# Relative attention over four batches: each tile's round trip to HBM in even and odd rows in place of column halves

## The chip, the cores and the metric

The program runs on one core of a Trainium2 chip. The metric is the device time of one execution in microseconds, from the first to the last instruction of that core, as a median over runs. The engines are TensorE (PE; its weight loads are PEld), VectorE (DVE), ScalarE (ACT), GpSimd (POOL), and SyncE (SP), which here only waits and issues DMAs.

## What is computed

Four batch elements of 2048 tokens with 256 channels pass through attention A, a feed-forward layer, attention B (causal) and the feed-forward layer again, each with a layer norm ahead and a residual sum behind. The change lies in attention A, which has 16 heads of 16 channels and a relative position score:

```python
content_score = einsum('bhsp,bhtp->bhst', q + u, k)
pos_score = einsum('bhsp,htp->bhst', q + v, pos)
x = pad(pos_score, ((0,0),(0,0),(0,0),(1,0)))          # a zero ahead of each row
pos_score = x.reshape(b, h, s + 1, s)[:, :, 1:, :].reshape(b, h, s, s)
weights = softmax((content_score + pos_score) / sqrt(P))
out = einsum('bhst,bhtp->bhsp', weights, val)
```

The relative shift is a change of row length: rows of 2049 floats (a zero and 2048 scores) are laid end to end, the first 2048 floats are dropped, and the rest is cut into rows of 2048.

## The kernel before, in words

One loop over the batch elements runs ten phases with a barrier between them; attention A is one of them. A head's 2048 x 2048 scores are worked in 16 tiles of 128 rows (`NT`), so a batch element has 256 tiles and the program 1024. On each engine `in_order` (line 491) writes out the steps by hand: step s works on several tiles at once, each part of the work some tiles ahead (`R_LEAD` 9, `Z_LEAD` 6, `C_LEAD` 4, `T_LEAD` 2, `V_LEAD` 1).

A tile n goes through these parts:

- **Position scores.** In step n-9, PE makes the 128 x 2048 scores in four matmuls of 512 columns (`rows_of`, line 516), in the order of columns 3, 0, 1, 2. DVE copies chunk 3 from PSUM into `rel` (line 693), ACT chunks 0, 1 and 2 (line 639). Each copy raises `r_copied[c]`. `rel` has four slots (`RING`).
- **Write.** In the same step SP writes the tile to `rel_rows` in HBM, in two DMAs of 512 KB (`write_half`, line 762). Row i of a head starts there at float i*2049 + 1, so that the row of 2049 with its zero comes about. Both DMAs raise `rel_out[slot]` by 16.
- **Read.** In step n-6 SP reads the shifted tile back into `z` (four slots), again as two DMAs of 512 KB (`read_half`, line 756); row i starts at float (i+1)*2048. Ahead of them `read_ready` (line 743) waits until the last transposes of tile n-4 have read the slot (`t_full[3]`, done by PE in this same step) and until both writes of tile n and of tile n+1 have landed. Both reads raise `rel_in[slot]`.
- **Scores.** In step n-4 PE makes the content scores, and DVE adds `z` and takes the maximum, in two halves (`score`, line 646; the custom instruction of line 658). It starts when both reads have landed. POOL subtracts the maximum (line 716).
- **Softmax and values.** In step n-2 PE transposes the tile (`turn`, line 538), ACT takes the exponential, and one step later PE multiplies with the values.

SP's queue is one order for everything: in a step it issues read half 0 of tile s+6, write half 0 of tile s+9, read half 1, write half 1 (`step`, lines 797 to 802), and behind them, in 12 of 16 steps, two loads of 64 KB for the next heads and in one step a load of 256 KB (`next_heads`, line 771; `load_part`, line 720, puts 16 rows into partitions six apart). A DMA that SP has not issued holds back all behind it. Before the change a half is 128 rows by 1024 columns: 128 pieces of 4 KB. Write half 0 waits for `r_copied[1]` (columns 0 to 1023), write half 1 for `r_copied[3]` and `r_copied[2]`:

```python
for c in ((R_DVE, R_ACT[-1]) if half else (R_ACT[1],)):
    e.wait_ge(r_copied[c], e.snap(base.tiles + (n + 1)))
```

PE waits for the same copies: its chunk 0 of the next tile's scores comes only after DVE's copy of chunk 3 (line 599), and DVE makes that copy behind its first half of `score`.

Two pieces of code outside of attention A come up below. At the start of the program the constant `embT` is loaded (128 partitions, two rows of 8 KB each), and then `k_sb` (zero there) is written from 48 partitions, 4 KB each, to two places of `qu_parts` and two of `k_parts`. Ahead of each attention A 24 loads of 64 KB fill the first heads' operands, by `load_part`.

Of the kernel before, what the change touches and what calls it, by code (L numbers as in the profile page):

```python
# [26 lines left out]
P = 128  # L27
# [4 lines left out]
S = 2048  # L32
NT = S // P
# [9 lines left out]
FLAT = S * (S + 1)  # L43
RING = 4
# [10 lines left out]
R_ACT = [0, 1, 2]  # L55
R_DVE = 3
R_FIRST = 3
HB = 4
NB = 2
# [20 lines left out]
def program(nc, a, out, nb=4, nh=H):  # L80

    ctx = ExitStack()
    with ctx:
        def sb(name, shape, dt=F32):
            return ctx.enter_context(nc.sbuf_tensor(name, shape, dt))
# [4 lines left out]
        def sem(name):  # L90
            return ctx.enter_context(nc.semaphore(name))
# [8 lines left out]
        rel_d = nc.dram_tensor("rel_rows", (NB, FLAT), F32).ap()  # L100
# [8 lines left out]
        rel = sb("rel", [P, RING, S])  # L109
        z = sb("z", [P, RING, S])  # L110
# [104 lines left out]
        r_copied = [sem(f"r_copied{c}") for c in range(4)]  # L215
        rel_out = [sem(f"rel_out{k}") for k in range(RING)]
        rel_in = [sem(f"rel_in{k}") for k in range(RING)]
# [13 lines left out]
        def settle(e):  # L231

            e.sem_inc(waited, 1)
# [257 lines left out]
        def in_order(e, b, step):  # L491

            def counts(p):
                return Counts(*(e.snap(b * (nh // HB * per) + p * per)
                                for per in (G, G // OB, 32 * G // RING, HB // NB * QK_INC, HB // NB * 16)))

            with e.Fori(0, 1) as p:
                base = counts(p)
                for s in range(-R_LEAD, 0):
                    step(p, base, s, lambda n: n >= 0)  # L500
            with e.Fori(0, GROUPS - 1) as p:
                base = counts(p)
                for s in range(G):
                    step(p, base, s, lambda n: True)
            with e.Fori(GROUPS - 1, GROUPS) as p:
                base = counts(p)
                for s in range(G):
                    step(p, base, s, lambda n: n < G)

        def moved(base, n):  # L510

            return base.moves + 32 * (n // RING + 1)
# [212 lines left out]
        def load_pair(e, q, k, q_src, k_src, h, slots, done):  # L725

            for a in slots:
                load_part(e, q, q_src, h, a, QPART[a], done)
                load_part(e, k, k_src, h, a, KPART[a], done)

        def load_v(e, h, hd, done):
            e.dma_start(v_s[hd].rearrange("p t w -> p (t w)"),
                        v_d[bass.ds(h, 1)].rearrange("a p w -> (a p) w")).then_inc(done, 16)

        def sp_attn_a(e, b):

            every = range(SLOTS)
            load_pair(e, qv_s[0], pos_s[0], qv_d, pos_d, 0, every, qv_loaded[0])
            load_pair(e, qu_s[0], k_s[0], qu_d, k_d, 0, every, AA["qk_loaded0"])
            load_v(e, 0, 0, AA["v_loaded0"])  # L740
            load_pair(e, qv_s[1], pos_s[1], qv_d, pos_d, 1, every, qv_loaded[1])

            def read_ready(p, base, n, fresh, last):

                k = n % RING
                if not fresh:

                    e.wait_ge(t_full[3], e.snap(base.tiles + (n - RING + 1)))
                    settle(e)
                e.wait_ge(rel_out[k], e.snap(moved(base, n)))  # L750
                settle(e)
                if not last:
                    e.wait_ge(rel_out[(n + 1) % RING], e.snap(moved(base, n + 1)))
                    settle(e)

            def read_half(n, half):

                k, hd, i0, c0 = n % RING, n // NT % NB, n % NT * P, half * S // 2
                shifted = bass.AP(tensor=rel_d.tensor, offset=hd * FLAT + (i0 + 1) * S + c0, ap=[[S, P], [1, S // 2]])
                e.dma_start(z[:, k, c0:c0 + S // 2], shifted).then_inc(rel_in[k], 16)  # L760

            def write_half(base, n, half):

                k, hd, i0, c0 = n % RING, n // NT % NB, n % NT * P, half * S // 2
                for c in ((R_DVE, R_ACT[-1]) if half else (R_ACT[1],)):
                    e.wait_ge(r_copied[c], e.snap(base.tiles + (n + 1)))
                    settle(e)
                there = bass.AP(tensor=rel_d.tensor, offset=hd * FLAT + i0 * (S + 1) + 1 + c0, ap=[[S + 1, P], [1, S // 2]])
                e.dma_start(there, rel[:, k, c0:c0 + S // 2]).then_inc(rel_out[k], 16)

            def next_heads(p, base, s, final):

                hd, at = s // NT, s % NT
                nxt = (hd + 1) % NB
                if at in range(1, 7) and not (final and hd + 1 >= HB):
                    if at == 1:
                        e.wait_ge(AA["hi_ready"], e.snap(base.tiles + hd * NT + C_LEAD))
                        settle(e)
                    load_pair(e, qu_s[nxt], k_s[nxt], qu_d, k_d, e.snap(p * HB + (hd + 1)), (at - 1,),
                              AA[f"qk_loaded{nxt}"])  # L780
                if at == 7 and not (final and hd + 1 >= HB):
                    e.wait_ge(AA["pv_done"], e.snap(base.tiles + (hd * NT + V_LEAD)))
                    settle(e)
                    load_v(e, e.snap(p * HB + (hd + 1)), nxt, AA[f"v_loaded{nxt}"])
                if at in range(8, 14) and not (final and hd + 2 >= HB):
                    if at == 8:
                        e.wait_ge(r_full[2], e.snap(base.tiles + (hd + 1) * NT))
                        settle(e)
                    load_pair(e, qv_s[hd % NB], pos_s[hd % NB], qv_d, pos_d, e.snap(p * HB + (hd + 2)), (at - 8,),
                              qv_loaded[hd % NB])  # L790

            def step(p, base, s, here):

                n, r = s + Z_LEAD, s + R_LEAD
                final = not here(G)
                if here(n):
                    read_ready(p, base, n, s < 0 and n < RING, n % NT == NT - 1)
                for half in range(2):
                    if here(n):
                        read_half(n, half)  # L800
                    if here(r):
                        write_half(base, r, half)
                if s >= 0:
                    next_heads(p, base, s, final)

            in_order(e, b, step)
# [642 lines left out]
```

## Time and profile before

| | |
|---|---|
| median of 3 runs | 11098.51 us (11085.86 to 11107.45) |
| profiled execution | 11115.23 us |
| its span, first to last instruction | 11113.4 us |
| busy share: PE, PEld, DVE, ACT, POOL | 85%, 60%, 56%, 60%, 26% |
| mean granted clock of TensorE | 0.947 |
| bytes moved by DMA | 2482 MB, 223 GB/s over the span |

The page of the profile is of one execution. Its rows give busy time by group of instructions, waits with what ended them, and for DMA the packets, their bytes and the share of time in which the core's 16 DMA engines had a packet under way; that share can come out a little over 100%, since a packet is counted as begun a few ns before the one ahead of it has ended. The profiled execution is 16.7 us above the median, and the same events make up both.

### The profile page before, as it was taken

The page shows a single profiled execution, that of the slowest core. Times are in us where ns is not written, and L with a number is a line of the kernel's source. Part 1 is how long each engine was busy: PE and PEld are TensorE (multiplying, and loading weights), DVE is VectorE, ACT ScalarE, POOL GpSimd, SP SyncE. Part 2 cuts the span into 40 slices and gives each one's busy share as a digit, 9 for nine tenths or more (in the row PEclk, how much of TensorE's full clock was granted, in tenths as well). Part 3 has the DMA queues.
Part 4 walks back from the last instruction along what each step waited for, and adds up shares of the span by engine and source line. Part 5 has one row for each costly group of instructions (what it writes and reads, how often), then busy time and mean ns, then how long its engine had stood idle before and what let it go on. Part 6 is the DMA issues. An engine that isn't in the chain of part 4 may idle for free. (4 is left out here: it accounts for less than half of the span.)

```text
span 11113.4 us, 271423 instructions
## 1 busy us (share of the span) xinstructions
PE 9422.7 (85%) x95520; PEld 6711.5 (60%) x95520; DVE 6258.0 (56%) x14730; ACT 6687.5 (60%) x11009; POOL 2944.3 (26%) x3520
## 2 busy tenths in 40 slices
PE   5888888999688888899968888889996888888999
PEld 3665665666465666566646656656663565665666
DVE  3655663765365566376446556637644565663764
ACT  3666663765466666376546666637644666663764
POOL 2333332001233333200123333310012333331001
PEclk7999999999899999999989999999998999999999
DMA  6999992000699999100069999911007999991100
GB/s 240 378 363 366 381 378 87 26 25 16 233 377 366 361 379 380 59 25 25 16 254 380 367 362 382 365 46 27 23 18 265 373 372 362 379 357 48 27 22 26
DMA packets 747623, 2482.45 MB, mean 223 GB/s; under 512 B 111745, under 2 KB 133761, under 8 KB 745921
## 3 DMA queue, kind: packets, MB, share of 16 engines
q1 hardware_dynamic: 746176, 2463.84, 60.3%
q8 instruction: 826, 13.53, 0.5%
q14 instruction: 621, 5.08, 0.1%
HBM read 1280.34 MB, written 1183.07 MB: 222 GB/s over the span
## 5 line engine op out<-in xcount | busy, mean ns | idle before, releaser
L658 DVE CUSTOM_DVE_ANT_0 z<-sc,z 128x1024 f32<-128x1024 f32 x2048 | 2496.5, 1220 | 1848.5 <-DMA z<-rel_rows 1608.0
L716 POOL TENSOR_SCALAR z<-z,nmax 128x1024 f32<-128x1024 f32 x2048 | 2277.8, 1123 | 4028.5 <-DVE nmax L668 4028.5
L631 ACT ACTIVATE pT<-rg 128x512 f32<-128x512 f32 x4096 | 2445.9, 598 | 738.7 <-PE rg L541 679.5
L541 PE MATMUL rg<-ident,z 128*128 128x128 f32 x16384 | 2527.0, 277 | 77.0 <-issue 68.3
L639 ACT ACTIVATE rel<-rg 128x512 f32<-128x512 f32 x3072 | 1721.1, 596 | 1407.2 <-PE rg L522 1401.8
L541 PEld LDWEIGHTS rg<-ident,z 128*128 128x128 f32 x16384 | 1990.3, 142 | 784.6 <-ACT rel L639 294.4
L522 PE MATMUL rg<-pos_s,qv_s 96*128 96x512 bf16 x4096 | 1590.8, 396 | 1021.4 <-DVE rel L693 901.6
L1013 DVE CUSTOM_DVE_ANT_0 z<-sc,mask 128x1024 f32<-128x1024 f32 (+7 forms) x1536 | 1359.1, 910 | 227.0 <-PE sc L832 173.9
L952 ACT ACTIVATE pT<-rg 128x512 f32<-128x512 f32 (+3 forms) x1792 | 928.4, 550 | 763.0 <-PE rg L885 751.0
L522 PEld LDWEIGHTS rg<-pos_s,qv_s 96*128 96x128 bf16 x4096 | 478.7, 118 | 1498.0 <-DVE rel L693 1150.9
L960 ACT ACTIVATE z<-z,nmax 128x128 f32<-128x128 f32 (+15 forms) x1024 | 1226.6, 1198 | 89.0 <-POOL nmax L978 76.7
L885 PE MATMUL rg<-ident,z 128*128 128x128 f32 x8704 | 1256.8, 289 | 0.0
L562 PE MATMUL op<-pT,xnT 128*32 128x128 f32 x32768 | 1129.9, 279 | 0.0
L885 PEld LDWEIGHTS rg<-ident,z 128*128 128x128 f32 x8704 | 972.0, 145 | 254.9 <-issue 188.4
L562 PEld LDWEIGHTS op<-pT,xnT 128*32 128x32 f32 x32768 | 847.2, 111 | 243.9 <-issue 214.0
L866 PE MATMUL op<-pT,xnT 128*32 128x128 f32 x17408 | 791.9, 283 | 149.6 <-ACT pT L952 45.5
L693 DVE COPY rel<-rg 128x512 f32<-128x512 f32 x1024 | 702.4, 686 | 183.1 <-PE rg L522 142.4
L866 PEld LDWEIGHTS op<-pT,xnT 128*32 128x32 f32 x17408 | 503.2, 110 | 299.1 <-DVE attn L988 120.6
L534 PE MATMUL sc<-k_sb,xnT 96*128 96x512 bf16 x2048 | 631.2, 390 | 0.0
L534 PE MATMUL sc<-xnT 96*128 96x512 bf16 x2048 | 615.1, 381 | 0.7 <-DVE mlo L658 0.7
L1032 DVE COPY pT<-rg 128x512 f32<-128x512 f32 (+3 forms) x768 | 428.6, 558 | 297.3 <-PE rg L885 288.2
L700 DVE COPY po_sb<-op 128x128 f32<-128x128 f32 x1024 | 298.8, 292 | 494.1 <-PE op L562 493.2
(93 smaller groups left out, 8161.5 us busy)
## 6 DMA issues: line engine op xcount, KB each, us to landing
rel_rows<-rel SPq DMA_DIRECT2D x2048, 512.0 KB, 7.2
z<-rel_rows SPq DMA_DIRECT2D x2048, 512.0 KB, 7.1
xnT<-qu_parts SPq DMA_DIRECT2D x792, 64.0 KB, 2.3
xnT<-v_heads SPq DMA_DIRECT2D x132, 256.0 KB, 4.3
v_heads<-rel SPq DMA_DIRECT2D x8, 4096.0 KB, 12.5
k_sb<-k_parts SPq DMA_DIRECT2D x408, 64.0 KB, 2.3
qv_s<-qv_parts SPq DMA_DIRECT2D x384, 64.0 KB, 6.2
pos_s<-pos_parts SPq DMA_DIRECT2D x384, 64.0 KB, 7.2
```

The lines of the kernel that those rows point to most:

```text
L522: e.matmul(rg[:, R_BANK[c], :], qv_s[hd][:, i0:i0 + P], pos_s[hd][:, c * CH:(c + 1) * CH], start=True, stop=True).then_inc(r_full[c], 1)
L534: mm = e.matmul(sc[:, c, :], qu_s[hd % NB][:, i0:i0 + P], k_s[hd % NB][:, c * CH:(c + 1) * CH], start=True, stop=True)
L541: mm = e.transpose(rg[:, T_BANK[q], (j - 4 * q) * P:(j - 4 * q + 1) * P], z[:, n % RING, j * P:(j + 1) * P], ident[:, :])
L562: mm = e.matmul(po[32 * g:32 * g + 32, :], v_s[hd % NB][:, j, :], pT[:, n % 2, j * P:(j + 1) * P], start=j < 4, stop=j + 4 >= NT)
L631: e.activation(pT[:, t % 2, q * CH:(q + 1) * CH], rg[:, T_BANK[q], :], ACT.Exp, scale=SCALE).then_inc(p_ready[q], 1)
L639: e.activation(rel[:, r % RING, c * CH:(c + 1) * CH], rg[:, R_BANK[c], :], ACT.Copy).then_inc(r_copied[c], 1)
L658: e.tensor_tensor_reduce(out=zs, in0=scf[:, 2 * half * CH:2 * (half + 1) * CH], in1=zs, scale=1.0, scalar=-3.0e38, op0=ALU.add, op1=ALU.ma ...
L716: e.tensor_scalar(zs, zs, 1.0, nmax[:, n % 2:n % 2 + 1], ALU.mult, ALU.add).then_inc(AA[done], 1)
L866: mm = e.matmul(po[32 * g:32 * g + 32, :], v_s[t // NT % NB][:, j, :], pT[:, t % 2, j * P:(j + 1) * P], start=j < 4, stop=j + 4 >= nj)
L885: mm = e.transpose(rg[:, B_BANK[q], (j - 4 * q) * P:(j - 4 * q + 1) * P], z[:, t % RING, j * P:(j + 1) * P], ident[:, :])
L960: e.activation(z[:, s % RING, 0:w], z[:, s % RING, 0:w], ACT.Exp, bias=nmax[:, s % 2:s % 2 + 1], scale=SCALE).then_inc(BB["exp_done"], 1)
L1013: e.tensor_tensor_reduce(out=z[:, s % RING, c0:c1], in0=scf[:, p0:p0 + c1 - c0], in1=mask[:, S - width + c0:S - width + c1], scale=1.0, sc ...
```

## The change

A half is no longer 1024 columns of all 128 rows but all 2048 columns of 64 rows: half 0 is the even rows of the tile, half 1 the odd ones, for the write and for the read. A DMA then has 64 pieces of 8 KB where it had 128 of 4 KB; it still carries 512 KB. Write half 0 now waits for the whole tile (`r_copied[3]` and `r_copied[2]`), write half 1 for nothing. The order in which SP issues them, the semaphores and their counts stay.

```diff
             def read_half(n, half):
 
-                k, hd, i0, c0 = n % RING, n // NT % NB, n % NT * P, half * S // 2
-                shifted = bass.AP(tensor=rel_d.tensor, offset=hd * FLAT + (i0 + 1) * S + c0, ap=[[S, P], [1, S // 2]])
-                e.dma_start(z[:, k, c0:c0 + S // 2], shifted).then_inc(rel_in[k], 16)
+                k, hd, i0 = n % RING, n // NT % NB, n % NT * P
+                shifted = bass.AP(tensor=rel_d.tensor, offset=hd * FLAT + (i0 + 1 + half) * S, ap=[[2 * S, P // 2], [1, S]])
+                e.dma_start(z[half:P:2, k, :], shifted).then_inc(rel_in[k], 16)
 
             def write_half(base, n, half):
 
-                k, hd, i0, c0 = n % RING, n // NT % NB, n % NT * P, half * S // 2
-                for c in ((R_DVE, R_ACT[-1]) if half else (R_ACT[1],)):
-                    e.wait_ge(r_copied[c], e.snap(base.tiles + (n + 1)))
-                    settle(e)
-                there = bass.AP(tensor=rel_d.tensor, offset=hd * FLAT + i0 * (S + 1) + 1 + c0, ap=[[S + 1, P], [1, S // 2]])
-                e.dma_start(there, rel[:, k, c0:c0 + S // 2]).then_inc(rel_out[k], 16)
+                k, hd, i0 = n % RING, n // NT % NB, n % NT * P
+                if half == 0:
+                    for c in (R_DVE, R_ACT[-1]):
+                        e.wait_ge(r_copied[c], e.snap(base.tiles + (n + 1)))
+                        settle(e)
+                there = bass.AP(tensor=rel_d.tensor, offset=hd * FLAT + (i0 + half) * (S + 1) + 1, ap=[[2 * (S + 1), P // 2], [1, S]])
+                e.dma_start(there, rel[half:P:2, k, :]).then_inc(rel_out[k], 16)
```

## Rows read from the trace of the kernel before

**Rows 1.** The page: packets of the whole span.

```profile
DMA packets 747623, 2482.45 MB, mean 223 GB/s; under 512 B 111745, under 2 KB 133761, under 8 KB 745921
```

**Rows 2.** Windows, the four stretches of attention A: times, busy, clock, DMA share, GB/s.

```profile
181.00:1696.00 1515.00, 1276.72 (x14597) 910.79 (x14597) 901.18 (x1894) 1002.25 (x1765) 562.74 (x506) 0.98 1.00 373
2935.00:4453.00 1518.00, 1283.67 (x14593) 915.67 (x14594) 901.01 (x1894) 1001.84 (x1765) 562.74 (x506) 0.97 1.00 372
5700.00:7210.00 1510.00, 1275.17 (x14593) 910.33 (x14594) 900.58 (x1894) 1001.78 (x1765) 562.80 (x506) 0.98 1.00 374
8467.00:9985.00 1518.00, 1278.43 (x14595) 911.89 (x14596) 900.99 (x1894) 1001.68 (x1765) 562.78 (x506) 0.97 1.00 373
```

**Rows 3.** Waits over the whole span: who waited for whom, us, times, longest.

```profile
DVE z L658 <- DMA z<-rel_rows: 1608.0, 905, 10.6
...
PE rg L522 <- DVE rel L693: 901.6, 989, 9.6
```

**Rows 4.** DMA, 200 to 1690 us: GB/s in 40 slices, packets, the queue.

```profile
GB/s 371 391 390 372 376 372 389 376 366 377 289 373 351 382 387 385 375 374 376 392 372 285 392 366 382 389 379 381 369 376 378 392 385 372 387 378 384 366 368 382
DMA packets 158334, 556.84 MB, mean 374 GB/s; under 512 B 21898, under 2 KB 21898, under 8 KB 158125
...
q1 hardware_dynamic: 158125, 554.14, 99.6%
```

**Rows 5.** DMA, 18 to 21 us: the load of embT, rows of 8 KB.

```profile
DMA packets 177, 1.25 MB, mean 418 GB/s; under 512 B 11, under 2 KB 25, under 8 KB 25
...
q1 hardware_dynamic: 177, 1.25, 100.4%
```

**Rows 6.** DMA, 182 to 185 us: writes of rel_rows alone, 4 KB each.

```profile
DMA packets 330, 1.22 MB, mean 407 GB/s; under 512 B 32, under 2 KB 32, under 8 KB 330
...
q1 hardware_dynamic: 330, 1.22, 101.7%
```

**Rows 7.** Timeline, one tile: start, us, what, idle before it.

```profile
1005.16 1.09 ACT L639 ACTIVATE rel<-rg 128x512 f32<-128x512 f32 x2 [1.15 <-PE rg L522]
...
1006.34 0.33 SPq L769 DMA_DIRECT2D rel_rows<-rel  x1
...
1006.72 0.61 SPq L760 DMA_DIRECT2D z<-rel_rows  x1
1006.85 0.60 ACT L639 ACTIVATE rel<-rg 128x512 f32<-128x512 f32 x1 [0.61 <-PE rg L522]
...
1007.54 0.62 SPq L769 DMA_DIRECT2D rel_rows<-rel  x1
...
1009.09 0.60 PE L541 MATMUL rg<-ident,z 128*128 128x128 f32 x4
...
1010.45 0.56 SPq L760 DMA_DIRECT2D z<-rel_rows  x1
...
1011.60 0.33 SPq L769 DMA_DIRECT2D rel_rows<-rel  x1
...
1012.80 0.78 SPq L769 DMA_DIRECT2D rel_rows<-rel  x1
```

**Rows 8.** DMA issues: count, KB each, median us to landing.

```profile
rel_rows<-rel SPq DMA_DIRECT2D x2048, 512.0 KB, 7.2
z<-rel_rows SPq DMA_DIRECT2D x2048, 512.0 KB, 7.1
xnT<-qu_parts SPq DMA_DIRECT2D x792, 64.0 KB, 2.3
...
qu_parts<-k_sb SPq DMA_DIRECT2D x2, 192.0 KB, 10.8
```

**Rows 9.** Line 760, the reads: landing times of all 2048.

```profile
DMA to landing us min/median/max: 3.8/7.1/9.9
```

**Rows 10.** DMA, 22.2 to 23.2 us: writes out of 48 partitions (k_sb).

```profile
DMA packets 120, 0.39 MB, mean 385 GB/s; under 512 B 28, under 2 KB 28, under 8 KB 112
```

**Rows 11.** DMA, 160 to 172 us: loads into 16 partitions, six apart.

```profile
q1 hardware_dynamic: 604, 1.24, 40.4%
```

## The prediction

> **What bounds the kernel now.** I read the page first. Its DMA row shows that nearly all packets are under 8 KB [rows 1], and its slices show four stretches in which the DMA engines are full and four in which they are nearly idle. So I took the windows of the four full stretches, which are attention A: 1515, 1518, 1510 and 1518 us, 6061 us in all, with a DMA share of 1.00 and 372 to 374 GB/s in each, while PE is busy for 84% at a granted clock of 0.97 to 0.98 [rows 2]. Over 1024 tiles that is 5.92 us a tile. The waits say that the DMA is also what ends last: DVE waited for the read of `z` ahead of line 658 in 905 tiles, 1608 us in all, and PE waited 901.6 us in 989 tiles for the copy that DVE makes behind that [rows 3]. TensorE would be faster by about 0.9 us a tile if the reads came at once. The reader is to see a closed loop: 99.6% of the time of 16 DMA engines is taken [rows 4], the queue is filled as far as the four slots of `z` and `rel` allow, and compute runs at the rate of the landings. So a cheaper byte shortens the stage, and a busier compute engine would not lengthen it.
>
> Half of the change acts on the price of a byte, the other half on when the DMAs are issued.
>
> **The pieces of 8 KB.** A tile moves 2 MiB (2.097 MB), a write and a read of 1 MiB; with the head loads it is 374 times 5.92, some 2.21 MB. The trace has both sizes of piece under a full queue. While `embT` is loaded, 152 of the 177 packets are 8 KB and they carry all of the 1.25 MB, at 418 GB/s [rows 5]; so a row of 8 KB is one packet and isn't cut in two. While `rel_rows` is written alone, in 4 KB pieces, it is 407 GB/s [rows 6]. That is 2.6% less time for a byte. The 2.097 MB take 5.61 us at 374 GB/s, and 2.6% of that is 0.148 us a tile.
>
> The bounds. The mixture of reads and writes runs at 374, not at 407 GB/s, and what takes the difference isn't in a row: 0.996 times 1490 us times 16 engines over 136,227 packets of over 512 B is 174 ns each [rows 4], against 48.8 us over 298 packets, 164 ns, in writes alone [rows 6]. If those 10 ns belong to the packet and not to its bytes, 16 packets fewer on each DMA engine and tile save 0.16 us more, 0.31 in all. If the mixture is bound by the memory behind the engines, the size of a piece gains nothing: 0. I take 0.148, nearest to the rows that show both sizes; nothing shows that the stalls go by the packet.
>
> The Trainium skill (DMA: Bandwidth & Descriptors, "Why small descriptors are slow (HBM only)") puts the fixed overhead of a packet inside a DMA engine at some 3 cycles, of a fabric of 850 MHz: 3.5 ns, so 16 fewer would save 0.06 us a tile. By it alone the gain here would be 58 us, not 151.
>
> **The later issue.** Write half 0 waited for columns 0 to 1023 and now waits for the last copy. In the timeline it is issued at 1006.34, behind ACT's first two copies (1005.16 to 1006.25), and write half 1 at 1007.54, behind the copy that runs from 1006.85 to 1007.45; one tile on it is 1011.60 and 1012.80 [rows 7]. So write half 0 moves back by 1.2 us. Queued behind it on SP are read half 1 (at 1006.72 now, so 1007.9), write half 1 (then 1008.5 or so), the two head loads of 12 steps in 16, and the next read half 0, which was issued at 1010.45 although its transposes (from 1009.09 for 0.60 us) had been done for 0.8 us; it will be some 1 us later. All four of a tile's DMAs so shift by up to 1.2 us against compute. DVE waits for the landing of read half 1, PE for DVE.
>
> What hides it is the queue. A DMA of 512 KB lands 7.1 us (median) after its issue; one of 64 KB outside of the stretch takes 2.3 us [rows 8]; 512 KB at 374 GB/s are 1.4 us. So some 3.4 us of older work stand ahead of a DMA when it is issued. With 1.2 us off, 2.2 us are left, and the engines go on without a gap. But this is a median: the reads land after 3.8 to 9.9 us [rows 9], and 3.8 is a queue with nothing in it. Where less than 1.2 us stands ahead, the engines will run dry.
>
> The bounds here: nothing, if the queue always covers it; and 0.6 us a tile, if the queue is used up. The latter: a slot of `z` comes round in four periods, of which two are compute behind the scores (n-4 to n-2), so that 1.2 us more in the loop would be borne by two periods. A gain is excluded, since nothing is issued sooner but by the one wait that SP saves, and SP has idle time. I take a price from the slices: 3 of the 40 are at 289, 351 and 285 GB/s where the rest are at 362 to 392 [rows 4], so in one tile of 13 the queue is short already; each of them pays 1.2 us, 0.09 us a tile.
>
> Costed at nothing: a DMA's issue on SP (four of a tile, 0.33 to 0.8 us each, no more pieces than before); the landings, since both halves of a read and both writes of tiles n and n+1 were waited for before as well; DVE, ACT, PE, POOL, whose instructions don't change. Cover for all is the DMA queue; were it gone, PE would be next, at about 5.0 us a tile.
>
> **The sum.** -0.148 + 0.09 = -0.058 us a tile, times 1024: -59 us. The profiled execution took 11115.2, 16.7 above the median of 11098.5; taken from the latter, 11040 us, 0.5% less. A change within 0.2%, 22 us, is about what can't be told from none.
>
> **Rivals.**
>
> *A: the stalls go by the packet.* Then it is -0.31 + 0.09 = -0.22 us a tile, -225 us: 10873. For it: a larger piece has fewer starts. Against it: the same 4 KB pieces, written alone, take 164 ns, so it is the mixture that stalls and not the start of a piece. 0.11.
>
> *B: the two terms cancel*, or the mixture is bound by memory and the queue covers the delay: 11077 to 11120. 0.19 with the flank of the forecast.
>
> *C: the delay decides.* The place is write half 0's wait on SP, with read half 1 behind it. Should half of the 0.6 us come through, it is +0.30 - 0.148 = +0.15 us a tile, +156: 11254. The point from which it turns: more than 0.148 us a tile, an eighth of the 1.2 us. For it: 16 DMA engines don't run evenly, and a landing waits for the last; the queue of the slowest tiles is empty now. Against it: 99.6%, and 3.4 us ahead in the median. 0.22.
>
> *D: half of the partitions.* A DMA now reads or fills every second partition. If DMA engines get in each other's way on the SBUF side, the price shows in two places. The writes out of 48 partitions ran at 385 GB/s [rows 10], so the writing half should be safe. The loads into 16 partitions six apart took 0.404 times 12 times 16, 77.6 us for 1.24 MB [rows 11], 62.6 ns for 1000 bytes against 40.0 in rows 6: 1.56 times. If that were all from sharing, and the reads (1.05 MB, 2.8 us a tile) took 1.56 times as long, it is +1.6 us a tile. But each of those loads is a single piece for a DMA engine on an empty queue, so a first access is in it; and four pieces an engine spread over more places. I take a quarter of it, 0.4 us: 11040 + 410 = 11450. It turns from 0.06 us, 2% of the reads' time. 0.15.
>
> *That 8 KB rows are cut in two*, so that the change isn't what it says, is excluded by rows 5.
>
> **How the numbers follow.** The forecast has 0.33 as a gain of over 0.2%, and A 0.11: faster 0.44. B gives same 0.19. C 0.22 and D 0.15: slower 0.37. The likeliest case's own range is 10945 to 11110 (a gain of 0.12 to 0.18 us a tile, a loss of 0.03 to 0.13). The range over the cases goes from A's 10873 to C's 11254; D and the outermost bounds are left out, 2 in 10.
>
> **What the profile after would show.** Packets of 8 KB in attention A, some 260,000 of them, and a mean GB/s of 376 to 380 in the four stretches at a DMA share still at 0.98 or more: the forecast. Write half 0 behind the third copy of line 639, and a median landing about 1 us shorter: the delay as told. A share down to 0.95 with the stage no shorter: C. A share still at 1.00 and GB/s well under 370: D, and the time per 8 KB packet far over 330 ns. GB/s near 390: A. I am wrong if the stage moves while the GB/s don't, or if PE's waits on DVE's copy don't follow the stage.

## The result: 4.7% slower, and the profile after

The changed kernel takes 11616.35 us (median; 11610.57 to 11665.41) against 11102.98 us before: a ratio of 1.0466, with a 95% interval of 1.0447 to 1.0484. That is 513 us more, where 59 us less was forecast.

All of it lies in attention A. The windows of its four stretches after (start:end, length, busy us with counts of PE, PEld, DVE, ACT and POOL, granted clock, DMA share, GB/s):

```profile
181.00:1826.00 1645.00, 1328.44 (x14609) 946.20 (x14609) 902.71 (x1898) 1005.82 (x1767) 562.93 (x507) 0.94 0.96 344
3075.00:4717.00 1642.00, 1331.64 (x14642) 949.70 (x14643) 904.18 (x1901) 1006.53 (x1768) 563.99 (x508) 0.94 0.96 345
5948.00:7587.00 1639.00, 1325.05 (x14644) 944.35 (x14645) 904.10 (x1902) 1006.21 (x1768) 564.11 (x508) 0.95 0.96 346
8829.00:10483.00 1654.00, 1343.44 (x14637) 957.67 (x14641) 904.52 (x1900) 1007.59 (x1768) 564.11 (x508) 0.93 0.96 342
```

These are 6580 us against 6061 [rows 2]. The windows of before end 4 to 6 us ahead of a stage's last landing, those of after at most 2, so a stage is better taken from the first issue of its DMAs of `rel_rows` to their last landing (from the trace): 6583 us against 6083, 500 us more, 6.43 us a tile for 5.94. The two profiled executions differ by 496 us. The DMA share is 0.96 where it was 1.00, the rate 342 to 346 GB/s where it was 372 to 374. The engines do the same work (DVE, ACT and POOL are busy as long as before); TensorE's mean granted clock is 0.93 to 0.95 where it was 0.97 to 0.98, and the same matmuls keep it busy for 4% longer (1328 us for 1277 in the first stretch); it waits longer than before all the same.

The DMA view of 200 to 1690 us after, and the waits over the span:

```profile
DMA packets 86786, 511.78 MB, mean 343 GB/s; under 512 B 20386, under 2 KB 20386, under 8 KB 27586
...
q1 hardware_dynamic: 86595, 509.30, 95.5%
```

```profile
DVE z L658 <- DMA z<-rel_rows: 1843.8, 820, 10.7
...
PE rg L522 <- DVE rel L693: 1186.9, 953, 9.7
```

The pieces are what the change says: of 86,786 packets only 27,586 are under 8 KB. But the engines have a packet under way for 95.5% of the time in place of 99.6% [rows 4], and the waits of PE behind the read have grown from 901.6 to 1186.9 us [rows 3].

The issues over the whole span (count, KB, median us from issue to landing), and all times of the reads:

```profile
rel_rows<-rel SPq DMA_DIRECT2D x2048, 512.0 KB, 6.6
z<-rel_rows SPq DMA_DIRECT2D x2048, 512.0 KB, 6.5
```

```profile
L760 SPq DMA_DIRECT2D z<-rel_rows x2048: 450/588/2194, 187.2 to 10478.2; - x187
...
DMA to landing us min/median/max: 3.7/6.5/9.0
```

The landing after the issue is 0.6 us shorter than before, 6.5 for 7.1 [rows 8]. And the issue itself is slower: at least 450 ns on SP, where the forms of 128 rows took at least 314 (shown below). In the timeline of one tile after, the issue order can be read off as in rows 7:

```profile
1008.93 0.52 SPq L760 DMA_DIRECT2D z<-rel_rows  x1
...
1009.41 0.60 ACT L639 ACTIVATE rel<-rg 128x512 f32<-128x512 f32 x1 [0.61 <-PE rg L522]
...
1010.10 0.49 SPq L770 DMA_DIRECT2D rel_rows<-rel  x1
...
1010.64 0.59 SPq L760 DMA_DIRECT2D z<-rel_rows  x1
...
1011.02 1.23 DVE L658 CUSTOM_DVE_ANT_0 z<-sc,z 128x1024 f32<-128x1024 f32 x1 [1.61 <-DMA z<-rel_rows]
...
1011.28 1.25 SPq L770 DMA_DIRECT2D rel_rows<-rel  x1
...
1012.17 0.69 DVE L693 COPY rel<-rg 128x512 f32<-128x512 f32 x1
...
1015.03 0.60 ACT L639 ACTIVATE rel<-rg 128x512 f32<-128x512 f32 x1 [0.61 <-PE rg L522]
...
1016.85 0.59 SPq L760 DMA_DIRECT2D z<-rel_rows  x1
```

Read half 0 is issued at 1008.93, then SP stands until ACT's last copy has ended (1010.01) and sends write half 0, read half 1 and write half 1 in one burst. The last three lines show what the wait hangs on: DVE copies chunk 3 behind its first half of `score` (1011.02), ACT's last copy ends 4.61 us after the start of that `score`, and only then does the next read half 1 go out.

### The profile page after: what moved, and what is told of

It is laid out like the page before. It is cut to its first block and busy times, and to the rows that moved or that the text cites. A ratio compares the mean times of both kernels' runs of the same rounds, so it can differ in the third digit from the quotient of the medians.

```text
span 11609.5 us, 270399 instructions
## 1 busy us (share of the span) xinstructions
PE 9622.3 (83%) x95520; PEld 6849.9 (59%) x95520; DVE 6257.9 (54%) x14730; ACT 6698.1 (58%) x11009; POOL 2939.1 (25%) x3520
## 5 line engine op out<-in xcount | busy, mean ns | idle before, releaser
L522 PE MATMUL rg<-pos_s,qv_s 96*128 96x512 bf16 x4096 | 1633.6, 406 | 1307.1 <-DVE rel L693 1186.9
L541 PE MATMUL rg<-ident,z 128*128 128x128 f32 x16384 | 2581.5, 281 | 86.1 <-issue 77.4
L541 PEld LDWEIGHTS rg<-ident,z 128*128 128x128 f32 x16384 | 2051.6, 145 | 816.4 <-ACT rel L639 262.5
L886 PE MATMUL rg<-ident,z 128*128 128x128 f32 x8704 | 1257.4, 289 | 0.0
L562 PE MATMUL op<-pT,xnT 128*32 128x128 f32 x32768 | 1215.2, 293 | 0.0
L886 PEld LDWEIGHTS rg<-ident,z 128*128 128x128 f32 x8704 | 971.8, 145 | 254.7 <-issue 188.1
L562 PEld LDWEIGHTS op<-pT,xnT 128*32 128x32 f32 x32768 | 903.9, 116 | 259.7 <-issue 209.0
L867 PE MATMUL op<-pT,xnT 128*32 128x128 f32 x17408 | 791.7, 283 | 149.5 <-ACT pT L953 45.5
L867 PEld LDWEIGHTS op<-pT,xnT 128*32 128x32 f32 x17408 | 503.1, 110 | 298.9 <-DVE attn L989 120.4
```

The source lines that it names most:

```text
L522: e.matmul(rg[:, R_BANK[c], :], qv_s[hd][:, i0:i0 + P], pos_s[hd][:, c * CH:(c + 1) * CH], start=True, stop=True).then_inc(r_full[c], 1)
L541: mm = e.transpose(rg[:, T_BANK[q], (j - 4 * q) * P:(j - 4 * q + 1) * P], z[:, n % RING, j * P:(j + 1) * P], ident[:, :])
L562: mm = e.matmul(po[32 * g:32 * g + 32, :], v_s[hd % NB][:, j, :], pT[:, n % 2, j * P:(j + 1) * P], start=j < 4, stop=j + 4 >= NT)
L867: mm = e.matmul(po[32 * g:32 * g + 32, :], v_s[t // NT % NB][:, j, :], pT[:, t % 2, j * P:(j + 1) * P], start=j < 4, stop=j + 4 >= nj)
L886: mm = e.transpose(rg[:, B_BANK[q], (j - 4 * q) * P:(j - 4 * q + 1) * P], z[:, t % RING, j * P:(j + 1) * P], ident[:, :])
```

## The experiments

Each kernel was timed against the kernel before on the same chip. There were two theories at the start: **delay** (what the new wait holds up costs the time) and **sharing** (DMA engines get in each other's way when every second partition is used). Once delay had held, the question was what part of it counts.

### Shapes alone, and each part alone

**b1_bench.** Ahead of the last constant load of the kernel before, eight blocks of 4 MiB, each alone on the queue:

```diff
+            for k in range(RING):
+                for h in range(2):
+                    move(flat(k * P + h, 2, P // 2, S, S), z[h:P:2, k, :])
+            landed()
...
+            for k in range(RING):
+                for h in range(2):
+                    move(z[h:P:2, k, :], flat(k * P + h, 2, P // 2, S, S))
+            landed()
```

> The kernel before, with eight blocks of DMAs ahead of its last constant load, each block of 4 MiB in itself and alone on the queue: first written to HBM, then read back, as column halves (128 pieces of 4 KB), even and odd rows (64 of 8 KB), upper and lower 64 rows (64 of 8 KB) and whole tiles (128 of 8 KB). Two theories. Sharing: DMA engines that fill or drain every second partition get in each other's way on the SBUF side. Then the reads in even and odd rows run well under those of column halves (at 350 GB/s or less against 400), those of 64 rows on end at about half, near 210, and whole tiles at 410 to 420; the writes may show it or not. Delay: the shape isn't at fault. Then every block runs at 395 to 420 GB/s, the ones of 8 KB pieces some 2% above column halves.

The DMA view inside the blocks, written first (column halves, even and odd rows, upper and lower 64, whole), then read in the same order:

```profile
DMA packets 1000, 3.64 MB, mean 404 GB/s; under 512 B 112, under 2 KB 112, under 8 KB 1000
```
```profile
DMA packets 576, 3.80 MB, mean 422 GB/s; under 512 B 112, under 2 KB 112, under 8 KB 112
```
```profile
DMA packets 593, 3.88 MB, mean 298 GB/s; under 512 B 120, under 2 KB 120, under 8 KB 120
```
```profile
DMA packets 504, 3.74 MB, mean 415 GB/s; under 512 B 48, under 2 KB 48, under 8 KB 48
```
```profile
DMA packets 1092, 3.99 MB, mean 363 GB/s; under 512 B 117, under 2 KB 117, under 8 KB 1092
```
```profile
DMA packets 621, 4.05 MB, mean 368 GB/s; under 512 B 127, under 2 KB 127, under 8 KB 127
```
```profile
DMA packets 624, 4.07 MB, mean 214 GB/s; under 512 B 127, under 2 KB 127, under 8 KB 127
```
```profile
DMA packets 550, 4.10 MB, mean 410 GB/s; under 512 B 50, under 2 KB 50, under 8 KB 50
```

These windows cut the blocks at different places; that of the even and odd reads takes in both idle ends of its block. From the first packet's start to the last one's end, worked out from the trace, the four shapes are written at 399, 413, 287 and 412 GB/s and read at 339, 358, 217 and 370. Either way even and odd rows are no slower than column halves. Sharing is there, but for another shape: 64 rows on end. So sharing falls as the cause. That each block would run at 395 to 420 GB/s, as delay had it, missed for all reads and for 64 rows on end. (This single execution took 11219.88 us, 111 us above the kernel before, about the time of the blocks.)

**e1_late_wait.** The waits alone; column halves stay.

```diff
-                for c in ((R_DVE, R_ACT[-1]) if half else (R_ACT[1],)):
-                    e.wait_ge(r_copied[c], e.snap(base.tiles + (n + 1)))
-                    settle(e)
+                if half == 0:
+                    for c in (R_DVE, R_ACT[-1]):
+                        e.wait_ge(r_copied[c], e.snap(base.tiles + (n + 1)))
+                        settle(e)
```

> Column halves as before; only the waits are those of the changed kernel (write half 0 waits for the whole tile, write half 1 for nothing). Delay: most of the loss of 513 us is here, 11400 to 11620 us. Sharing: only the 0.09 us a tile of the prediction, 11100 to 11200 us.

Measured 11483.23 us against 11109.11, ratio 1.0326 (1.0291 to 1.0361): 374 of the 513 us with no change of shape. Delay holds.

**e2_read_rows.** Reads in even and odd rows, nothing else.

```diff
...
-                e.dma_start(z[:, k, c0:c0 + S // 2], shifted).then_inc(rel_in[k], 16)
+                e.dma_start(z[half:P:2, k, :], shifted).then_inc(rel_in[k], 16)
```

> Only the reads are even and odd rows; the writes are column halves with the early wait. Delay: no loss, since nothing is issued later: 11000 to 11110 us. Sharing on the side that fills SBUF: 11400 to 11620 us.

Measured 11065.45 us, ratio 0.9956 (0.9943 to 0.9970): 0.4% faster. The half of the change that adds no wait is a gain.

**e3_write_rows.** Writes in even and odd rows with their late wait, reads as before.

```diff
...
-                e.dma_start(there, rel[:, k, c0:c0 + S // 2]).then_inc(rel_out[k], 16)
+                e.dma_start(there, rel[half:P:2, k, :]).then_inc(rel_out[k], 16)
```

> Only the writes are even and odd rows, with the late wait; the reads are column halves. Delay: 11400 to 11620 us. Sharing on the side that fills SBUF: 11050 to 11200 us. Should it be slow while the column halves with the late wait are not, the writes share too.

Measured 11643.94 us, ratio 1.0476 (1.0439 to 1.0513). That is a little above both ranges. With the late wait the row writes add 161 us to e1. With the gain of the row reads, 44 us by e2, the parts come to 374 + 161 - 44 = 491 of the 513 us.

### What is late: the write or the read behind it

Write half 0's wait holds up the write, and read half 1 behind it on SP. Four orders of issue tell which counts.

**e8_cols_late_reads_first.** e1 with both reads issued first; **e7_rows_reads_first**, the same edit on the changed kernel; **e10_before_reads_first**, on the kernel before.

```diff
                 for half in range(2):
                     if here(n):
                         read_half(n, half)
+                for half in range(2):
                     if here(r):
                         write_half(base, r, half)
```

> Column halves with the late wait (11483 us in the run before), but SP issues both reads first and then both writes, so that only the writes stand behind the wait. Theory 1, the late read: the loss comes from read half 1 queued behind write half 0's wait; then it goes, 11050 to 11200 us. Theory 2, the late write: the pause ahead of write half 0 and the burst behind it drain the queue whatever the order; then it stays at 11400 us or more.

Measured 11102.34 us against 11121.49, ratio 0.9990 (0.9976 to 1.0004). The late wait is still there and costs next to nothing (this order without the late wait, e10 below, is 0.13% better by its ratio, about 15 us): the 374 us were read half 1 standing behind it.

> The changed kernel with both reads issued ahead of both writes. Late read: 11000 to 11200 us, and a little under the column halves in this order, by the larger pieces. Late write: 11500 us or more. If it stays some 150 us above the column halves in this order, the writes in even and odd rows have a cost of their own.

Measured 11000.10 us, ratio 0.9896 (0.9877 to 0.9916): the changed kernel, with its reads out of the way of the wait, is 1.0% faster than before, and 102 us under e8. Here the size of the pieces shows by itself.

> The kernel before, early wait and column halves kept, with both reads issued ahead of both writes. Late read: read half 1 gains 1.5 to 2 us against compute, but the DMA engines were already full, so little is left to gain: 11050 to 11130 us. If a full queue still left stalls in the reads, it is 11000 us or less; if alternating reads and writes had a worth of its own, 11150 us or more.

Measured 11078.94 us against 11113.10, ratio 0.9977 (0.9964 to 0.9989). Sooner than before brings next to nothing; later costs much.

**e9_read1_last.** The kernel before, both of its waits kept, read half 1 issued last.

```diff
-                for half in range(2):
-                    if here(n):
-                        read_half(n, half)
+                if here(n):
+                    read_half(n, 0)
+                for half in range(2):
                     if here(r):
                         write_half(base, r, half)
+                if here(n):
+                    read_half(n, 1)
```

> The kernel before, both early and late waits kept, with read half 1 issued behind write half 1 in place of between the writes: the read is late by 0.8 to 1.6 us and no write is later. Late read: 11300 to 11600 us. Late write: 11050 to 11200 us.

Measured 11961.10 us, ratio 1.0754 (1.0731 to 1.0776). No write is later behind its `score` than before, and the loss is the largest of these orders, 840 us, above what was expected of either theory. The late read is shown from both sides. The DMA view of its 200 to 1690 us:

```profile
DMA packets 138892, 487.56 MB, mean 327 GB/s; under 512 B 19442, under 2 KB 19442, under 8 KB 138708
...
q1 hardware_dynamic: 138708, 485.18, 98.9%
```

This is the row to remember: a share of 98.9% at 327 GB/s, where before it was 99.6% at 374 [rows 4]. The same pieces take longer: 0.989 times 1490 us times 16 engines over the 119,266 packets of over 512 B is 198 ns each, for 174 before. In e3, where the size tells the direction, it is the reads that are stretched: from 300 to 1600 us its 4 KB packets, all of them reads (some 4,800 of 55,700 are loads for the next heads), took 199 ns in the mean, and its 8 KB writes 325, so 162 for 4 KB (means worked out from the trace's packets). A packet counts as under way while it is stretched, so a full share doesn't say that the queue holds work in advance.

### How much, by how late

**e13_read_ahead_of_write.** Column halves; read half 1 behind the wait, but ahead of write half 0. `write_ready` is the late wait of e1, taken out of `write_half`.

```diff
+                if here(n):
+                    read_half(n, 0)
+                if here(r):
+                    write_ready(base, r)
+                if here(n):
+                    read_half(n, 1)
                 for half in range(2):
-                    if here(n):
-                        read_half(n, half)
                     if here(r):
                         write_half(base, r, half)
```

> Column halves; read half 1 still behind the wait for the last copy, but issued ahead of write half 0. It comes 0.38 us sooner than with the late wait alone, and with 512 KB less ahead of it on the queue. Late read, by time of issue alone: a third of 374 us less, 11330 to 11420 us. If the write ahead of it on the queue is what it waits for: 11150 to 11300 us. If the wait alone is the matter: 11483 us still.

Measured 11317.13 us against 11116.04, ratio 1.0181 (1.0158 to 1.0204), between the two ranges given.

**e12_late_and_pause.** e1 with a pause on SP behind write half 0.

```diff
+                if half == 0:
+                    for _ in range(6):
+                        settle(e)
```

> Column halves with the late wait (11483 us), and six more semaphore increments on SP between write half 0 and read half 1, a pause of some 0.3 us that moves nothing but the issues behind it. It stands for the slower issue of the 64-row forms, which in the run with the writes in even and odd rows puts read half 1 later by some 0.3 us. If the lateness of read half 1 is all of that run's 160 us above the late wait: 11580 to 11720 us. If the 8 KB writes cost something of their own: 11480 to 11540 us.

Measured 11550.75 us, ratio 1.0385 (1.0362 to 1.0407): 67 us over e1, under the one range and 11 us over the other.

For these runs I worked out of the trace, for the tiles between 300 and 1600 us, the mean time from the start of DVE's first half of `score` to the end of SP's issue of read half 1 in the same step, and the time from there to the `score` that this read feeds, which is two tiles on. The two add up to two periods (the time of a tile), by construction; what the table shows is how a later issue is shared out between them. The loss is that against the kernel before, timed beside it:

| run | `score` to issue of read half 1 | from there to its own `score` | period | loss |
|---|---|---|---|---|
| e10, reads first | 3.54 us | 8.21 us | 5.88 us | -34 us |
| e8, reads first, late wait | 3.64 us | 8.30 us | 5.97 us | -19 us |
| before | 4.41 us | 7.51 us | 5.96 us | 0 |
| e13 | 5.14 us | 7.29 us | 6.21 us | 201 us |
| e1 | 5.71 us | 6.94 us | 6.32 us | 374 us |
| e12 | 6.00 us | 6.84 us | 6.42 us | 435 us |
| e3 | 6.17 us | 6.87 us | 6.52 us | 535 us |
| changed kernel | 6.21 us | 6.74 us | 6.48 us | 513 us |
| e9 | 6.04 us | 7.54 us | 6.79 us | 840 us |

A read that is issued 0.8 to 0.9 us sooner than before (e10, e8) lands sooner by next to nothing: the second column grows by 0.7 to 0.8. One that is issued later makes up for less than half of it: e1 is 1.30 us later and wins back 0.57, and half of the 0.73 left is 0.365 us a tile, 374 us. The runs from e13 down to the changed kernel cost 274 to 304 us for each microsecond of later issue. e9 is off this line, at 515: it is 1.63 us later and wins back nothing. It has both writes ahead of the late read; no run shows whether that is the reason.

The first column hangs on compute. ACT's last copy ends 4.61 us (median) after the start of `score` in every run of the table; where the late read stands behind that copy, `score`, the copies, SP's issue and the landing are one closed loop of two periods. TensorE's clock goes into its length. In e1, 31 of the 206 tiles had a matmul of the position scores that took over 500 ns, at the lower of the clock's two levels; ACT's last copy ended 5.5 us behind `score` there, not 4.6, and the issue of read half 1 at 6.44 us, that of the others at 5.58. Before, it is 13 of 218 tiles. No run takes the clock apart from the wait.

**e14_rows_read_ahead.** e13's order on the changed kernel.

> The changed kernel, all in even and odd rows, with read half 1 issued behind the wait for the last copy but ahead of write half 0 (the same with column halves: 11317 us). If 8 KB pieces are cheaper wherever the read is in time, and the writes in rows cost only by standing ahead of the late read, it is at or under that, 11200 to 11320 us. If writes in rows have a cost of their own once the read is late, 11360 us or more.

Measured 11200.64 us against 11122.86, ratio 1.0068 (1.0051 to 1.0084): 1.1% under the same order in column halves, so row writes have no cost of their own that shows. In e3 and in the changed kernel they cost because write half 0 stands between the wait and the late read, and SP takes longer over it: the issue of read half 1 ends 0.46 us later in e3 than in e1, which at the 274 to 304 us above is some 130 of the 161 us. A part of that is the issue of the write itself; the issues of e1 and of the changed kernel's form in e3 (min, median, max ns):

```profile
L770 SPq DMA_DIRECT2D rel_rows<-rel x2048: 314/448/1643, 180.5 to 10366.0; - x187
```
```profile
L770 SPq DMA_DIRECT2D rel_rows<-rel x2048: 450/516/2329, 180.2 to 10507.9; - x187
```

The 64-row form takes 136 ns more at the least. It goes by the number of rows and not by their length or the step: whole tiles of 128 rows by 8 KB were issued in 314 ns too (e6), 64 rows on end, without the step of two, in 460 (e4).

### A kernel that beats both

**e5_read_whole.** The kernel before with a tile's reads made one DMA.

```diff
+                if half:
+                    return
...
+                e.dma_start(z[:, k, :], shifted).then_inc(rel_in[k], 16)
```

> The kernel before, with the two reads of a tile made one of 128 rows by 8 KB (1 MiB), issued where read half 0 was; writes as before. Late read: the read is complete on the queue 2.2 us sooner and has the larger pieces (-0.4% in the run with the reads in even and odd rows), so 10950 to 11070 us. Late write: as that run, 11020 to 11110 us. Should the alternation of halves matter by itself, it is above 11150 us.

Measured 11023.30 us against 11121.49, ratio 0.9907 (0.9889 to 0.9924). That lies in the ranges of both theories and doesn't tell them apart.

**e11_whole_read_row_writes.** The same read, and the changed kernel's writes.

> The read of a tile as one DMA of 1 MiB ahead of the writes, and the writes in even and odd rows with the late wait: all pieces 8 KB, nothing to be read stands behind the wait. Late read, with the larger pieces as a gain: 10930 to 11030 us, at or under the changed kernel with its reads first (11000 us). Late write: above 11100 us.

Measured 10967.18 us against 11113.10, ratio 0.9866 (0.9842 to 0.9890): the fastest. Its DMA view from 300 to 1600 us:

```profile
DMA packets 80196, 493.60 MB, mean 380 GB/s; under 512 B 16106, under 2 KB 16106, under 8 KB 23114
...
q1 hardware_dynamic: 80011, 491.20, 98.4%
```

The share is 98.4%, below that of before, at 380 GB/s.

**e6_whole_both.** One write of 1 MiB too.

```diff
...
+                there = bass.AP(tensor=rel_d.tensor, offset=hd * FLAT + i0 * (S + 1) + 1, ap=[[S + 1, P], [1, S]])
+                e.dma_start(there, rel[:, k, :]).then_inc(rel_out[k], 16)
```

> One read and one write of 1 MiB for a tile, 128 rows by 8 KB, the write behind the late wait. If only the read's place and the size of the pieces count: 10930 to 11050 us, as the run beside it. If the halving of the write matters, because the next read waits for the landing of both writes of the next tile, it is 11100 us or more.

Measured 11508.45 us, ratio 1.0359 (1.0336 to 1.0383), as slow as with a late read, but the read isn't late behind `score`: its issue ends 3.36 us behind it in the mean, in e11 3.21. SP's own waits from 200 to 1600 us (us, times, longest), e6 first, e11 second:

```profile
SPq L233 <- DMA rel_rows<-rel: 430.6, 196, 5.9
```
```profile
SPq L233 <- DMA rel_rows<-rel: 104.8, 104, 3.4
```

`read_ready` waits for the landing of the next tile's write, and a write of 1 MiB lands later (10.7 us in the median, where e11's halves take 7.9). The loop then goes through the write: from `score` to the write's issue 4.82 us, to its landing 10.61, to the read's issue 0.28, to the read's own `score` 9.38 (means from the trace), 25.1 us in all, which is four periods; in e11 the same way takes 23.4. No run took this wait out, so that it is the cause is read from the trace and not shown by a run.

**e4_top_bottom_rf.** e7 with the upper and the lower 64 rows as halves.

```diff
...
-                e.dma_start(z[half:P:2, k, :], shifted).then_inc(rel_in[k], 16)
+                e.dma_start(z[half * (P // 2):(half + 1) * (P // 2), k, :], shifted).then_inc(rel_in[k], 16)
```

> The changed kernel with its reads first (11000 us), but its halves are the upper and the lower 64 rows in place of even and odd ones. Alone on the queue these ran at 287 GB/s written and 217 read against 413 and 358 for even and odd rows. Sharing on the SBUF side: the mixture falls from 379 to between 250 and 330 GB/s, 11800 to 13500 us. If reads and writes in alternation hide it: under 11300 us.

Measured 12558.31 us, ratio 1.1311 (1.1283 to 1.1339), against 0.9896 for even and odd rows. So sharing is dear in the kernel too where the shape has it, and even and odd rows don't have it.

## Why the prediction was wrong

**The direction.** Faster was forecast, with 0.37 on slower; 11616 lies above the range. The time came from rival C, to which I gave 0.22 and 156 us.

**The bound of the stretch** was read rightly in one way: the reads' landing ends last, and the loop passes what it costs to PE. It was read wrongly in another: that 99.6% of the engines' time was taken, "the queue is filled", and so a shift of the issue would be hidden. e9 has 98.9% at 327 GB/s.

**The pieces of 8 KB: right in direction, too large by 29 to 48%.** I priced them at -0.148 us a tile, -151 us. With the read in time they brought 102 us (e8 to e7), with the read half late 117 (e13 to e14), in reads alone 44 (e2). The estimate from the overhead of a packet that the Trainium skill gives (DMA: Bandwidth & Descriptors, "Why small descriptors are slow (HBM only)"), 58 us, is too low, by 43 to 50%. Rival A isn't seen.

**The later issue: the step that failed.** "What hides it is the queue", with 3.4 us ahead and 1.2 us taken off, priced at 0.09 us a tile. The wait alone measures 374 us, 0.365 a tile (e1). The 3.4 us were the median landing less that of a quiet load, and I took all of it for older work that can be used up. The landing of reads tells how much really was: it went from 7.1 [rows 8] to 6.6 us in e1:

```profile
rel_rows<-rel SPq DMA_DIRECT2D x2048, 512.0 KB, 6.9
z<-rel_rows SPq DMA_DIRECT2D x2048, 512.0 KB, 6.6
```

So of 1.2 us later only 0.5 came back as a shorter landing, and the rest reached DVE. For read half 1 alone the table has 1.30 us later, 0.57 back and 0.73 left, and spread over two periods that is the 374 us. The cover was mis-sized, since a minimum of 3.8 us [rows 9] was the sign that I set aside as rare.

The upper bound of 0.6 us a tile held, but its loop was the wrong one, and that the factor of two came out is luck. I had the slot of `z` come round in four periods, two of them compute. But in the changed kernel SP hardly waits for that slot (`t_full[3]`, PE's line 541). Its waits for it (us, times, longest), first before, from 180 to 1695 us, then in the changed kernel, from 200 to 1600 us:

```profile
SPq L233 <- PE rg L541: 137.2, 124, 6.0
```
```profile
SPq L233 <- PE rg L541: 17.4, 12, 6.6
```

The loop that closes is `score`, DVE's copy of chunk 3, PE's chunk 0 of that same tile (not of the next, as I wrote ahead), ACT's copies, SP, the read, and the `score` two tiles on: a late read holds up the very copy that the next late read waits for.

The price of 0.09 us had no ground either. Two of the three low slices of [rows 4] fall on single pauses of 14 us, where the loop over groups of 64 tiles turns (tile 68's `score` starts at 604.7 us, 14.57 after the one ahead; tile 132's at 991.0, 14.08 after it), and tell nothing of a short queue in one tile of 13.

**"Costed at nothing: a DMA's issue on SP".** This was wrong too: 450 ns at the least in place of 314. By the table the later issue of read half 1 accounts for some 130 of the 161 us between e1 and e3. A pause on SP, 0.29 us of later issue, costs 67 (e12), and e14 shows no such cost where the write isn't ahead of the read.

**Rival D: excluded for this shape**, by the blocks (422 and 368 GB/s) and by e7. Why the loads six apart [rows 11] were dear, no run told. The Trainium skill (SBUF — State Buffer, "Door 1: The DMA port swizzle") gives some 218 GB/s for 64 partitions on end: the reads agree with 214, the writes ran at 298 and don't. What I had worked out from its rule for even and odd rows, reads twice as long, is not seen.

**Of the signs given** the one for C was right: a share of 0.955 with the stage no shorter. The landing was to be 1 us shorter and is 0.6; had I asked what follows from anything less than 1.2, the rival would have had its price.

## What to carry to other kernels

Before a DMA is put behind a longer wait, look at what is queued behind it on the same issuing engine, above all a read that compute waits for: move such reads ahead of the wait, and the same change can turn from a loss of 4.7% into a gain of 1.0%. A DMA share near 100% isn't a reserve; take the change in issue-to-landing time as the measure of what the queue absorbs, and price the rest by how many periods the loop has to bear it. To find that loop, follow the wait back to the instruction that it hangs on: here it was a copy behind the very `score` that the read feeds, and not the buffer's slot.

## What the runs showed of the hardware that I had not expected

The DMA share hardly follows the rate: 98.9% at 327 GB/s in e9, 98.4% at 380 in e11. Over a whole block of 4 MiB, alone on the queue (b1), reads run at 339 GB/s in pieces of 4 KB from 128 rows, at 358 in even and odd rows and at 370 in whole rows of 128; writes run at 399, 413 and 412. 64 partitions on end are read at 217 and written at 287. And SP takes longer to issue fewer rows: at least 450 ns for 64, 314 for 128.
